# Output loads of the last stage issued up to four strips later instead of up to two, with three output buffers

## What is computed

```python
x = x + conv_of_signs(_gn(x), kernel)            # layer 0
# layer 1, on y = _gn(x)
xc = y * ca_gate                                 # gate per image and channel
x2 = xc * (sigmoid(ssm(mean_c xc)) + sigmoid(conv7x7(feat)))   # gate per pixel
mean, var = x2.mean((0, 1, 2)), x2.var((0, 1, 2))
x = x + relu((x2 - mean) * rsqrt(var + EPS) * bn_gamma + bn_beta)
```

## Time and profile before

| what | us |
|---|---|
| median of 3 runs | 3292.24 |
| the three runs | 3287.10, 3292.24, 3293.02 |
| the profiled execution's own time | 3285.82 |
| its span, first to last instruction | 3284.0 |
| stage 4 in it | from about 2330 to the end |

### The profile page before, as it was taken

The page is one execution under the profiler, slowest core; times in us unless marked ns, Lnnn a source line. Parts: engine busy times, 40 slices in busy tenths (PEclk is TensorE's granted clock), DMA queues, the critical chain, the costliest instruction groups (busy, mean ns, idle before and its releaser), DMA issues. The chain is left out here.

```text
span 3284.0 us, 50167 instructions
## 1 busy us (share of the span) xinstructions
PE 2531.5 (77%) x17105; PEld 1633.0 (50%) x17105; DVE 2971.8 (90%) x4057; ACT 2701.3 (82%) x3772; POOL 57.1 (2%) x111
## 2 busy tenths in 40 slices
PE   7899999999999999999987333333566766667776
PEld 5566666666666666666442000000455555555555
DVE  8789998999988999889986899999999999999997
ACT  6788888888888888888774688888799888888887
POOL 3000000000000000000001200000000000000000
PEclk9999999999999999999998555555688878787777
DMA  8899999999999999999866699999599999999998
GB/s 315 321 374 409 376 369 371 373 409 382 368 365 372 406 383 371 367 365 395 280 171 169 264 421 421 420 421 418 236 429 428 429 429 428 429 429 429 429 429 363
DMA packets 199097, 1228.49 MB, mean 374 GB/s; under 512 B 29792, under 2 KB 38936, under 8 KB 157644
## 3 DMA queue, kind: packets, MB, share of 16 engines
q1 hardware_dynamic: 195884, 1223.41, 92.4%
q0 software_dynamic: 2976, 2.00, 0.3%
HBM read 805.14 MB, written 420.17 MB: 373 GB/s over the span
## 5 line engine op out<-in xcount | busy, mean ns | idle before, releaser
L1449 PE MATMUL psum<-signs,taps 128*128 128x448 f16 x4032 | 856.5, 355 | 40.7 <-DVE signs L1078 31.8
L1568 PE MATMUL psum<-signs,picked 12*128 12x448 bf16 x896 | 314.5, 491 | 340.7 <-DMA signs<-gate_scratch 271.0
L1449 PEld LDWEIGHTS psum<-signs,taps 128*128 128x128 f16 x4032 | 385.2, 98 | 367.2 <-DVE signs L1078 51.3
L2001 DVE SCALAR_TENSOR_TENSOR xc<-xt,curs,psum 128x1792 f32<-128x1792 f32 x222 | 452.1, 2078 | 57.0 <-PE psum L1568 45.5
L841 ACT ACTIVATE xt<-psum 128x896 f32<-128x896 f32 x416 | 377.9, 910 | 143.6 <-PE psum L1347 129.7
L1781 DVE SCALAR_TENSOR_TENSOR xc<-xt,curs,psum 128x1792 f32<-128x1792 f32 x224 | 455.8, 2079 | 33.3 <-PE psum L1568 32.3
L1710 ACT ACTIVATE xc<-xc 128x1792 f32<-128x1792 f32 x224 | 380.1, 1697 | 95.2 <-DVE xc L1781 95.2
L1129 DVE CUSTOM_DVE_ANT_0 xt<-work,xt 128x896 f32<-128x896 int8 x416 | 436.0, 1086 | 13.7 <-ACT work L849 13.6
L1347 PE MATMUL psum<-ident,stage 128*128 128x128 f32 x3066 | 410.6, 276 | 22.0 <-DMA stage<-x_dram 12.3
L1972 ACT ACTIVATE xc<-xc,bn,curs 128x1792 f32<-128x1792 f32 x224 | 411.7, 1903 | 13.8 <-DVE xc L2001 4.7
L857 ACT ACTIVATE work<-xt,mean 128x1792 bf16<-128x1792 f32 x208 | 370.2, 1780 | 29.2 <-DVE x1max_p L1129 29.2
(11 more groups left out here) (221 smaller groups left out, 2953.2 us busy)
## 6 DMA issues: line engine op xcount, KB each, us to landing
xt<-x_scratch SPq DMA_DIRECT2D x210, 1792.0 KB, 25.3
stage<-x_dram SPq DMA_DIRECT2D x219, 896.0 KB, 10.0
xc<-x_scratch SPq DMA_DIRECT2D x210, 896.0 KB, 9.3
x_scratch<-xt SPq DMA_DIRECT2D x208, 896.0 KB, 9.3
out_dram<-stage SPq DMA_DIRECT2D x75, 1792.0 KB, 21.9
out_dram<-work SPq DMA_DIRECT2D x37, 1792.0 KB, 21.9
x_scratch<-last_unit SPq DMA_DIRECT2D x16, 896.0 KB, 10.2
signs<-ssm_scratch SPq DMA_DIRECT2D x14, 448.0 KB, 4.7
```

Source lines behind the costliest of these rows:

```text
L1449: return nc.tensor.matmul(turn[h % 2][:, b * 512:b * 512 + HB], taps[:, j, t, :], signs[:, j, r:r + RT // 2, dw:dw + W], start=t == 0, sto ...
L1568: last = nc.tensor.matmul(dst[:, b, :], picked[:, b * P:(b + 1) * P], gate_rows[:, s * BW:(s + 1) * BW], start=True, stop=True)
L2001: nc.vector.scalar_tensor_tensor(quarters(xc[m % 2][:, j, :]), slot_quarters(s, j), curs[:, h, j:j + 1], gate_quarters(gate_ps4), ALU.add, ...
```

## The change

The load of strip f is issued up to four strips after its slot is free, in place of up to two. Nothing else is changed.

```diff
 def behind(m):
-    return min((m - NS) * 5 // (TOTAL - NS), 2)
+    return min((m - NS) * 5 // (TOTAL - NS), 4)
```

## The result

The changed kernel takes 3307.69 us (median of 5 runs, 3304.28 to 3316.93) against 3288.56 us before (5 runs, 3286.28 to 3293.02). The ratio is 1.0071, 95% interval 1.0057 to 1.0086: slower by 0.71%, some 19 us by the medians and 23 by the ratio. The forecast had the sign, and 7 us. The profiled execution is the slowest of the five, 3316.93 us, so it shows the mechanism larger than the median does.

A forecast was written before the change was run, and what follows sets the result against it. The prediction took stage 4 to be bound by a full DMA queue. A tail loss of 6.65 us plus 0.5 before it, say 7, on a median of 3292.24 gave 3299.2 us; range 3293 to 3308.

The forecast's parts named there:

- the line: Stage 4's queue of loads and stores: each lands when all issued before it have, some 4.35 us apart.
- R1: Rival, faster: the stores' landing is the bound, not the queue's rate; strips from 70 on gain, -18 us, 3274; chance 0.07.
- (a): Strips 70 and 91, each skipped turn: DVE waits once by about 4.35 us, queue two transfers shorter, no cost at the end.
- (c): The tail: load 111 lands two transfers later, four stores (17.4 us) hide a 24.05 us chain; 6.65 us lost, bounds 5.8 to 8.
- the order's 8.7 us: At the tail: load 111 goes out behind store 107 instead of 105, so lands two transfers, 8.7 us, later.
- the forecast 6.65: At the tail: idle queue time, 24.05 us of chain less 17.4 us of stores, makes the end 6.65 us later.
- (b): Strips 91 to 111, loads one turn ahead: the queue stays full; loss 0.5 us, bounds 0 to 6.
- R3: Rival, clearly slower: strips 91 to 111 take 9.9 us each as stores enter right before loads; 3324, half 3310; chance 0.14.
- R2: Rival, no measurable difference: tail of 5.8 us and nothing before it (3298.0), or a slightly faster short queue (3293.7); chance 0.35.

The follow-up runs named there:

- the middle part alone: The changed kernel with the last ten loads again issued as in the kernel before: 3297.11 us against 3285.41, ratio 1.0037.
- the slow VectorE: The kernel before with one more VectorE instruction of 2.02 us per strip, its result unread: 3448.85 us.

## Why the prediction was right and wrong

What bounds the kernel: right. The stage is bound by the line, ACT's waits for stores vanished and gave nothing (R1), and DVE's waits for loads took their place, one of some 5 us at the step.

(a) The step at strip 70: half right. Loads of 75 to 89 took 20 us and not 17, those from 92 on a median of 10.3 and not 9, because each transfer took longer. The line was shorter by what was skipped, as said.

(c) The tail: right, 24.2 us measured for 24.05, and the order's 8.7 us with it. With the last seven loads alone the whole kernel lost 8 to 11.5 us for the forecast 6.65.

(b) is the step that failed: "I take 0.5", with bounds 0 to 6, for a line that is short but full. Measured: 26.5 us in the profiled execution; and by the ratio of the middle part alone 0.37%, 12 us. Its test of whether transfers are issued in time was sound: in the turns 84 to 104 a load is issued 0.4 us after the sum and a store a median of 5.9, within that step's 4.6 to 7.0. What it took as fixed was the service time, 4.35 us. I had read 6.65 us for a lone transfer and 4.35 for one in the deep line and put the difference down to a constant 2.3 us around the service. The runs split it otherwise: with little ahead of it a store takes 5.7 to 6.3 us in most cases, some 1.5 around its 4.35, and a load 6.6 to 6.8, with more of it service, because its packets themselves are slower. The earlier trace rows could have warned: the first load went into an idle line, and the row that gave 6.6 could not say how much of it was service (the first store's 6.7 could not either). With the 1.5 us that only the later runs gave, a bound for a short line would have been 6.6 - 1.5 = 5.1 for a load, an estimate: 0.75 x 42 = 31 us.

R3 had 3310 to 3324 and a landing pace over 4.4 us as its mark, which came true (9.29 to 9.52 a pair), but not its mechanism: in the turns 84 to 104 only 3 of 21 stores went out later than its 6.7 us after the sum, and none after more than 7.0. R2 and R1 have fallen.

The forecast's 3299.2 is 8.5 us under the measured median; the range, 3293 to 3308, just holds it. The size of the effect was missed by a factor of about three: the sign and the tail were right for the reasons given, the loss before the tail was not foreseen. That the range still holds the median is luck in part: the upper bounds of (b) and (c) together, 6 and 8, end at 3306, and the kernel before, run five times, has a median 3.7 us lower than the 3292.24 that the forecast starts from.

The rule named there, of the Trainium skill, DMA: Bandwidth & Descriptors, section Rules for kernel authors (issue a DMA early, wait late), agrees with every kernel here whose `behind` goes over 2: each is slower, by 0.35 to 3.1%. I had let the rows overrule it where they showed only a deep line.

## What to carry to other kernels

This DMA-bound stage wants its queue deep, not just never empty: loads issued one turn ahead cost some 0.75 us a strip, and two turns ahead anything from nothing to nearly that, with the engines counted as busy for nearly all of the time, and nothing was gained in return. Read the rate beside the busy share; a share of 0.99 at 389 GB/s is a slower service, not a full one. And count the transfers left after the last load: as long as they cover the chain from that load to the end (24.2 us here, against 26.1 us of stores before the change and 17.4 after it), the tail costs nothing more, and below it the difference is lost. A landing is that of the slowest of the 16 DMA engines; look at the others too before calling a queue long.

## What the runs showed of the hardware

- One of the 16 DMA engines falls behind the others by about 0.1 us a pair in the kernel before, up to 10 us over the stage, and sets the landings (a second one is 5.7 us behind the median at load 100): 8.70 us a pair by the landings, 8.56 by the rate of 429 GB/s. In the changed kernel it is 13.3 us behind at load 80 and 1.2 at load 94, once the line is short enough for it to catch up. Without the small gate loads (12 partitions, 10.5 KB) the kernel before is 6 us faster. The Trainium skill, DMA: Bandwidth & Descriptors, section Latency and other measured facts, knows of two engines that are usually slower and guesses at transfers issued from GpSimd; here nearly all go out from SP, and the queue list on the page of the changed kernel's profile, below, has 2 MB of 1228 on the software queue, so that guess does not fit this case. Which engines they are the trace does not say, so they need not be the two of that section.

```profile
q1 hardware_dynamic: 195884, 1223.41, 92.3%
q0 software_dynamic: 2976, 2.00, 0.3%
```

- SP's own instruction for a load takes 0.35 us in the deep line and a median of 1.03 in the changed kernel from 2946 to 3072, where it directly follows a gate load:

```profile
L1909 SPq DMA_DIRECT2D xt<-x_scratch x14: 420/1033/1192, 2948.0 to 3071.4; - x14
```

With the slow VectorE it takes 0.61 (median of 78), and 0.34 without the gate loads. It costs the landing at most 0.1 us there (7.6 against 7.5).
